# Softmax maxima taken off by one product per head, and expert results kept in the order of the tokens' place in SBUF, on one Trainium2 core

## The chip, the cores and the metric

One core of one Trainium2 chip runs the whole program in one launch. The metric is the device time of that launch in microseconds; of the kernel before there are three runs, and the median counts.

## The reference

The input `x` is (2, 1024, 128) in f32. It passes a pre-norm attention block and a pre-norm mixture of experts, each added to its input.

- Attention: layernorm, RMS norm with a weight, then q, k and v for 16 heads of 8. One half of the output is causal linear attention over features of q and k of degree two, `y / (z + eps)`. The other half is softmax attention in which query t sees the keys t-64 to t. Both halves are joined and multiplied by `Wout` (256 x 128).
- Experts: layernorm, 8 gate logits, the top two experts per token with softmax weights. An expert computes `z = (x W1 + b1) * (x W2 + b2)`, `o = silu(z Wg + bg) * (z Wl + bl)`, `y = o W3 + b3`; the token's result is the weighted sum of its two experts' y.

## The kernel before

The 2048 tokens are 16 chunks of 128 (`NC`), chunk c holding tokens 128 c to 128 c + 127, one per partition: `x_all[p, c]`. After a stage of norms and projections, in which q and k are written to DRAM split into bf16 parts, there are two stages.

**Attention** goes chunk by chunk, each of four units (`u`; heads 8 at a time, window half `j = u // 2`, head half `hf = u % 2`). All five engines have hand-written streams with waits on semaphores. For each unit TensorE issues, in this order (`chunk`, from L624):

- L638: the products that update the linear attention's state (not in the last chunk of a sequence);
- L602: next unit's window scores with queries on the output's partitions, 8 products, for the maxima only. VectorE reduces them (L1098) to `mrow`: 128 partitions x 4, partition 64 r + q and column pr holding the maximum of head 2 pr + r and query q;
- `post`: the tail of the chunk before. In a chunk's first unit these are transposes of its outputs (L555, L557), which wait until ACT has copied them out of PSUM (L838, L839); later the product with `Wout` (L580, L581), the gate (L583) and places in the experts' lists (L541, L542);
- L655: the unit's scores again, now with keys on partitions, 8 products of 64 columns into bank ST, and onto them L659: minus the maxima;
- L673 and L678: linear attention. L678 waits for the squared scores that ACT makes (L818) and POOL masks (L1305);
- L614, L621: next unit's linear scores, and sums for the features;
- L690: after ACT has taken the exponential (L830) of bank ST, the products with v.

The maxima reach bank ST as a product because a value per column must be the same on all partitions. VectorE's `maxima` (L1093 to L1108) makes two bf16 parts of `-mrow`: `mneg[:, b, 0]` by L1105, the rounded value, and `mneg[:, b, 1]` by L1107, what the rounding lost. L659 then multiplies, for each of the four columns pr and each part, one column of `mneg`, repeated 128 times as weights, with a 128 x 128 identity; column k of the output gets `mneg[k]`, so 128 columns are the 64 queries of two heads. That is 4 x 2 = 8 products of 128 columns per unit, 512 in all.

VectorE, in the same chunk, does divisions, the second layernorm and the routing (`post`, from L1018): top two experts of each token (L1057 to L1074), one-hot rows (L1084), `member` (L1088), and `weights_row`, which writes into a token's row its weights and the number of the row where the result is to go (L1000): `tokid` for the first expert and `tokid + N` for the second (L986). POOL, besides the masks, multiplies features (L1260) and scatters the tokens' rows to DRAM, each to its expert's region of `routed` (L1266), two scatters per chunk. The first of them is issued in the chunk's last unit.

**Experts**: 39 tiles of 128 rows (`NT = 39`; each expert has at least one, and 31 are placed by a table that VectorE computes after the last token is routed, L1151 to L1171). `run_steps` fixes the order: tiles 0 to 7 are the first tiles of experts 0 to 7, the other 31 follow by the table. SP loads a tile's rows (`load_tile`), after the eighth tile only when the table is there and the regions' ends are padded (L470). Per step the engines work on five tiles at once: TensorE L720 to L753, VectorE L1188 to L1217, ACT L860 to L879. POOL scatters a tile's 128 weighted results as rows of 512 B into `results` (L1327), a tensor of two halves of N = 2048 rows. VectorE takes a slot's row numbers anew (L1216, L1217) only after the scatter that used it has landed.

**The end**: SP waits for all scatters (L475), issues eight loads of 256 KB (L479; four groups of four chunks, both halves), VectorE adds the two halves (L1223) and then `x_all` (L1225), and SP stores each group (L482).

## Time and profile before

| | |
|---|---|
| median of three runs | 466.5 us (466.21, 466.5, 468.2) |
| the profiled execution | 469.27 us, of which span 467.1 us |
| attention's units | from about 50 to 271 us |
| routing's last rows, table, first tiles | about 271 to 311 us |
| experts | to 452 us |
| last scatter's landing, loads, additions, stores | 453.5 to 467.1 us |

A line of the timeline is a group of instructions merged where they follow each other: start, length, engine, line, operation, tiles, count, and in brackets how long the engine was idle before it and what ended that. A line of waits is: who waited (engine, tile, line) for whom, us in total, how often, the longest. PE is TensorE's matmuls, PEld its weight loads, DVE is VectorE, SPq and POOLq are the parts of those engines that issue DMAs. The names in tiles are the program's tensors; `qas` also stands for the buffers that share its memory later (`og`, `oT`, `z`, `yw`), `ks` for `res`.

### The profile page before, as it was taken

What the parts mean: (1) busy time and instruction counts of PE and PEld (TensorE: products, weight loads), DVE (VectorE), ACT (ScalarE), POOL (GpSimd) and SP (SyncE); (2) the same over time, 40 slices, a digit from 0 to 9 for tenths busy, and PEclk for the clock granted to TensorE, in tenths of its full rate; (3) what the DMA queues carried; (4) which work ended last, traced back from release to release, by engine and by line L of the source; (5) the groups of instructions that cost most, each with busy time, mean ns of one, the idle gap of its engine ahead of it and who ended that gap; (6) DMA issues with size and microseconds to landing.
All of it is one profiled execution on the core that took longest, in us unless ns stands there. A gap on an engine that the chain in (4) does not pass through costs nothing. (4 is left out here: it accounts for less than half of the span.)

```text
span 467.1 us, 14166 instructions
## 1 busy us (share of the span) xinstructions
PE 392.9 (84%) x4805; PEld 265.0 (57%) x4805; DVE 292.8 (63%) x1150; ACT 204.0 (44%) x470; POOL 177.9 (38%) x305
## 2 busy tenths in 40 slices
PE   0877998999999999999999931799999999999930
PEld 0455676777766777767677620355555555555510
DVE  5566554678756877766766646267666666666614
ACT  0456454554554555554554610143444444444410
POOL 5263533454454564465553353012222222222220
PEclk9999999999999999999999975699999999999965
DMA  7548976555575555333324600201111111111008
GB/s 212 134 123 171 194 176 108 134 152 142 155 160 129 138 147 145 105 77 72 79 56 150 174 27 25 82 25 48 39 38 33 32 35 37 34 32 37 17 20 254
DMA packets 91623, 46.13 MB, mean 99 GB/s; under 512 B 56410, under 2 KB 89852, under 8 KB 91554
## 3 DMA queue, kind: packets, MB, share of 16 engines
q1 hardware_dynamic: 88562, 40.51, 34.7%
q0 software_dynamic: 2272, 4.46, 2.9%
q8 instruction: 40, 0.66, 0.6%
q10 hardware_dynamic: 720, 0.26, 0.2%
q14 instruction: 29, 0.24, 0.2%
HBM read 33.69 MB, written 11.98 MB: 98 GB/s over the span
## 5 line engine op out<-in xcount | busy, mean ns | idle before, releaser
L1327 POOL DMA_INDIRECT results<-qas,mrowid x39 | 38.1, 978 | 124.6 <-ACT qas L879 121.7
L1305 POOL TENSOR_SCALAR_AFFINE_SELECT amat<-amat 128x512 f32<-128x512 f32 x64 | 40.6, 635 | 108.9 <-ACT amat L818 108.6
L1098 DVE TENSOR_REDUCE mrow<-ps 128x4 f32<-128x512 f32 x64 | 44.1, 688 | 58.2 <-PE ps L602 58.0
L746 PE MATMUL ps<-wgl,rest 128*128 (+1 forms) x156 | 75.7, 608 | 2.8 <-DVE hT L1188 2.1
L830 ACT ACTIVATE pmat<-ps 128x512 f32<-128x512 f32 x64 | 38.2, 597 | 68.8 <-PE ps L659 68.8
L818 ACT ACTIVATE amat<-ps 128x512 f32<-128x512 f32 x64 | 38.2, 597 | 13.8 <-PE ps L614 10.6
L1188 DVE TENSOR_TENSOR hT<-ps,kv_tok 128x512 f32<-128x512 f32 x39 | 27.0, 691 | 26.5 <-PE ps L746 15.5
L731 PE MATMUL ps<-w,rest 128*128 (+1 forms) x78 | 41.9, 620 | 0.0
L746 PEld LDWEIGHTS ps<-wgl,rest 128*128 128x128 f32 x156 | 27.1, 193 | 26.0 <-issue 25.7
L659 PE MATMUL ps<-identb,mneg 128*128 128x128 bf16 x512 | 39.2, 219 | 0.0
L1266 POOL DMA_INDIRECT routed<-routed_row,slot x32 | 32.6, 1018 | 14.7 <-issue 5.8
L879 ACT ACTIVATE qas<-rest,mweight 128x128 f32<-128x128 f32 x39 | 15.7, 402 | 50.3 <-DVE rest L1205 50.3
L738 PEld LDWEIGHTS ps<-kv_tok,qas 128*128 128x128 f32 x156 | 23.6, 194 | 20.1 <-issue 20.0
L1260 POOL TENSOR_TENSOR phik<-u_tok 128x128 f32<-128x128 f32 (+3 forms) x112 | 33.4, 329 | 0.0
L1200 DVE TENSOR_TENSOR hT<-ps,b 128x512 f32<-128x512 f32 x39 | 26.7, 684 | 8.0 <-PE ps L731 8.0
L1193 DVE TENSOR_TENSOR qas<-qas,hT 128x256 f32<-128x256 f32 x39 | 16.6, 425 | 21.1 <-ACT qas L873 21.1
L659 PEld LDWEIGHTS ps<-identb,mneg 128*128 128x128 bf16 x512 | 29.7, 98 | 0.0
L638 PE MATMUL ps<-v,phik 128*96 128x18 f32 x224 | 28.7, 243 | 0.4 <-POOL phik L1260 0.4
L690 PE MATMUL ps<-pmat,v 128*32 128x64 f32 x1024 | 27.6, 225 | 0.6 <-ACT pmat L830 0.4
L602 PE MATMUL ps<-ks,qas 114*64 114x128 bf16 x512 | 26.5, 225 | 1.4 <-issue 1.4
L868 ACT COPY rest<-ps 128x384 f32<-128x384 f32 (+2 forms) x41 | 19.0, 463 | 18.8 <-PE ps L724 18.8
L690 PEld LDWEIGHTS ps<-pmat,v 128*32 128x32 f32 x1024 | 17.2, 109 | 17.2 <-ACT pmat L830 14.2
(161 smaller groups left out, 821.5 us busy)
## 6 DMA issues: line engine op xcount, KB each, us to landing
qa_parts<-wgl SPq DMA_DIRECT2D x12, 256.0 KB, 3.2
ks<-k_parts SPq DMA_DIRECT2D x32, 96.0 KB
qas<-qa_parts SPq DMA_DIRECT2D x32, 96.0 KB
xin<-routed SPq DMA_DIRECT2D x39, 72.0 KB, 1.9
ks<-k_parts SPq DMA_DIRECT2D x32, 64.0 KB
qas<-qa_parts SPq DMA_DIRECT2D x32, 64.0 KB
w<-in_W SPq DMA_DIRECT2D x2, 1024.0 KB, 5.7
wgl<-in_Wg SPq DMA_DIRECT2D x2, 1024.0 KB, 6.2
```

The source lines that it names most:

```text
L638: t = mm(ps[0:PR, KV, 2 * at * UD:2 * (at + 1) * UD], phik[:, p, 2 * at:2 * at + 2, :].rearrange("p h f -> p (h f)"), v1[:, p, 1, j, :].re ...
L659: t = mm(ps[:, ST, pr * CH:(pr + 1) * CH], mneg[:, u % 2, part, pr:pr + 1].to_broadcast([128, 128]), identb[:], start=False, stop=(part == ...
L690: t = mm(ps[32 * g:32 * g + 32, bank, at:at + WINDOW], slot32(v1[:, p, j], 8 * hf + hh), pmat[:, u % 2, hh, :], start=False, stop=True, sk ...
L731: mm(ps[:, X12, :], zxT[:, (k + 1) % 2, 2, :], rhs(w12[:, bass.ds(expert(1), 1), :]), start=True, stop=True).then_inc(x12_ready, 1)
L746: t = mm(ps[:, GL, :], zxT[:, k % 2, s, :], rhs(wgl[:, bass.ds(e, 1), s, :]), start=(s == 0), stop=(s == 1))
L818: a_(amat[:, u % 2].rearrange("p g t -> p (g t)"), ps[:, A, :], ACT.Square).then_inc(square_done, 1)
L830: a_(pmat[:, u % 2].rearrange("p g t -> p (g t)"), ps[:, ST, :], ACT.Exp).then_inc(exp_done, 1)
L1098: v.tensor_reduce(mrow[:], ps[:, SQ, :].rearrange("p (a k) -> p a k", k=CH), AX.X, ALU.max).then_inc(max_done, 1)
L1260: t = q.tensor_tensor(phik[:, p, :, at:at + w], u_tok[:, :, 0:w], u_tok[:, :, dl:UD], ALU.mult)
L1266: q.indirect_dma_start(routed, bass.IndirectOffsetOnAxis(slot[:, b, k:k + 1], 0), routed_row[:, b, :], None).then_inc(scattered[b], 16)
L1305: q.affine_select(out=amat[:, u % 2], in_=amat[:, u % 2], compare_op=ALU.is_ge, fill=0.0, base=0, pattern=[[0, 4], [1, CH]], channel_multi ...
L1327: q.indirect_dma_start(results, bass.IndirectOffsetOnAxis(mrowid[:, m:m + 1], 0), yw[:, m, :], None, bounds_check=RESULTS - 1, oob_is_err= ...
```

## The change

Maxima: `mneg` is now indexed by buffer, column pr and half r, with 128 partitions. The rows of a column (pr, r) hold, on the 64 partitions of half r, the rounded maxima of head 2 pr + r, and on the other 64 what the rounding lost. One product with `minusid`, two negated 64 x 64 identities on top of each other, adds both parts for one head: eight products of 64 columns per unit. VectorE makes `mneg` by two copies and two subtractions, each on 64 partitions, of which the subtractions write to the other half.

Results: `tokid` is now 16 p + c instead of 128 c + p, so the rows of `results` have the order of `x_all`'s places, partition by partition. A token's row in the second half is now the one for the expert with the higher number (`higher`), no longer the one for its second choice.

Tiles: 0 to 6 are the first tiles of experts 0 to 6, the table's 31 follow, and the last tile (38) is the first tile of expert 7. The wait for the table and for the padding comes one tile earlier.

End: SP waits for all scatters but the last tile's, loads half 0 in four loads, waits for the last, loads half 1 in four. VectorE adds half 0 to `x_all` by groups, then half 1.

```diff
--- before.py
+++ after.py
@@ -83,7 +83,7 @@
     valid[::T // CH, :, :WINDOW] = BIG
     c["iota8"] = np.tile(np.arange(E, dtype=np.float32), (128, 1))
     c["region0"] = np.tile(np.arange(E, dtype=np.float32) * REGION, (128, 1))
-    c["tokid"] = (np.arange(CH)[:, None] + CH * np.arange(NC)[None]).astype(np.float32)
+    c["tokid"] = (NC * np.arange(CH)[:, None] + np.arange(NC)[None]).astype(np.float32)
     pad = np.zeros((CH, ROW), np.float32)
     pad[:, D + E:] = TOPK * N + np.arange(CH)[:, None]
     c["padrows"] = pad
@@ -94,7 +94,7 @@
     c["sums"] = sums.reshape(KR, 2 * PR).astype(bf)
     c["qrows"], c["arows"], c["krows"] = (x.reshape(KR - KP, H * CH).astype(bf) for x in (qrows, arows, krows))
     c["valid"] = valid.reshape(NC, H * CH).astype(bf)
-    c["identb"] = np.eye(128, dtype=np.float32).astype(bf)
+    c["minusid"] = np.tile(-np.eye(WINDOW, dtype=np.float32), (2, 1)).astype(bf)
     return c
 
 
@@ -124,7 +124,7 @@
         results = dram("results", (RESULTS, D))
 
         ident = sb("ident", [128, 128])
-        identb = sb("identb", [128, 128], BF16)
+        minusid = sb("minusid", [128, WINDOW], BF16)
         sums = sb("sums", [KR, 2, PR], BF16)
         blockdiag = sb("blockdiag", [D, D])
         statemask = sb("statemask", [PR, 8 * UD])
@@ -167,7 +167,7 @@
         v1 = sb("v1", [CH, 2, 2, 2, SLOTW])
         state = sb("state", [PR, 2, 2, CH])
         mrow = sb("mrow", [128, 4])
-        mneg = sb("mneg", [128, 2, 2, 4], BF16)
+        mneg = sb("mneg", [128, 2, 4, 2], BF16)
         phiq = sb("phiq", [PR, 2, 4, CH])
         amat = sb("amat", [CH, 2, 4, CH])
         pmat = sb("pmat", [CH, 2, 8, WINDOW])
@@ -195,6 +195,7 @@
         top = sb("top", [CH, 8])
         topi = sb("topi", [CH, 8], mybir.dt.uint32)
         topf = sb("topf", [CH, 2])
+        higher = sb("higher", [CH, 1])
         onehot = sb("onehot", [CH, 2, E])
         member = sb("member", [CH, E], BF16)
         gap = sb("gap", [CH, 1])
@@ -280,7 +281,7 @@
          oT_copied, y_ready, y_added, y_weighted) = (sem(n) for n in (
              "tzx_ready", "zx_copied", "x12_ready", "x12_added", "z_ready", "meta_copied", "gl_ready", "gl_added",
              "silu_done", "o_ready", "to_ready", "oT_copied", "y_ready", "y_added", "y_weighted"))
-        res_in = [sem(f"res_in{g}") for g in range(NG)]
+        res_in = [[sem(f"res_in{k}{g}") for g in range(NG)] for k in range(2)]
         res_sum, out_sum = sem("res_sum"), sem("out_sum")
 
         TZX, X12, Y, TO, GL = SQ, ST, A, PHI, OUT0
@@ -317,12 +318,12 @@
 
             def expert_of(t):
 
-                if t < E:
-                    return t
+                if t < E - 1 or t == NT - 1:
+                    return min(t, E - 1)
                 if t not in known:
-                    if t == E:
+                    if t == E - 1:
                         engine.wait_ge(table_ready, 1)
-                    known[t] = engine.value_load(table[0:1, 0, t - E:t - E + 1], min_val=0, max_val=E - 1)
+                    known[t] = engine.value_load(table[0:1, 0, t - E + 1:t - E + 2], min_val=0, max_val=E - 1)
                 return known[t]
 
             known = {}
@@ -366,7 +367,7 @@
                 sp.dma_start(as_[KP:KR, p], con["arows"]).then_inc(s_in, 16)
                 for w in range(2):
                     sp.dma_start(ks[KP:KR, p, w], con["krows"]).then_inc(s_in, 16)
-            for dst, name in ((identb, "identb"), (sums, "sums"), (statemask, "statemask"), (epslin, "epslin")):
+            for dst, name in ((minusid, "minusid"), (sums, "sums"), (statemask, "statemask"), (epslin, "epslin")):
                 sp.dma_start(dst[:].rearrange("r a f -> r (a f)") if name == "sums" else dst[:], con[name]).then_inc(c_in, 16)
 
             def router_in():
@@ -455,28 +456,33 @@
                 if j >= 4:
                     sp.wait_ge(tzx_ready, j - 1)
                     sp.wait_ge(meta_copied, j - 3)
-                if j < E:
-                    row = j * REGION
+                if j < E - 1 or j == NT - 1:
+                    row = min(j, E - 1) * REGION
                 else:
-                    row = sp.value_load(table[0:1, 1, j - E:j - E + 1], min_val=0, max_val=E * REGION)
+                    row = sp.value_load(table[0:1, 1, j - E + 1:j - E + 2], min_val=0, max_val=E * REGION)
                 sp.dma_start(xin[:, k, :], routed[bass.ds(row, CH), :]).then_inc(xin_ready[k], 16)
 
             for j in range(4):
                 load_tile(j, j)
             pad_regions(sp)
-            for j in range(4, E):
+            for j in range(4, E - 1):
                 load_tile(j, j % 4)
             sp.wait_ge(table_ready, 1)
             sp.wait_ge(padded, 16 * (E + 1))
-            for j in range(E, NT):
+            for j in range(E - 1, NT):
                 load_tile(j, j % 4)
 
+            def load_results(half):
+                for g in range(NG):
+                    at = slice(g * GC, (g + 1) * GC)
+                    sp.dma_start(res[half][:, at], results[half * N:(half + 1) * N].rearrange("(p c) d -> p c d", c=NC)[:, at]).then_inc(res_in[half][g], 16)
+
+
             for k in range(4):
-                sp.wait_ge(y_out[k], 16 * ((NT - k + 3) // 4))
-            for g in range(NG):
-                for k in range(2):
-                    lo = k * N + g * GT
-                    sp.dma_start(res[k][:, g * GC:(g + 1) * GC], results[lo:lo + GT, :].rearrange("(c p) d -> p c d", p=CH)).then_inc(res_in[g], 16)
+                sp.wait_ge(y_out[k], 16 * ((NT - 1 - k + 3) // 4))
+            load_results(0)
+            sp.wait_ge(y_out[(NT - 1) % 4], 16 * ((NT - 1) // 4 + 1))
+            load_results(1)
             for g in range(NG):
                 sp.wait_ge(out_sum, g + 1)
                 sp.dma_start(out.rearrange("b (c p) d -> p (b c) d", p=CH)[:, g * GC:(g + 1) * GC], x_all[:, g * GC:(g + 1) * GC]).then_inc(done, 16)
@@ -654,10 +660,9 @@
                         h = 8 * hf + hh
                         mm(ps[:, ST, hh * WINDOW:(hh + 1) * WINDOW], ks[:, p, j, h, :], qs[:, p, h, j * WINDOW:(j + 1) * WINDOW],
                            start=(hh == 0), stop=False, skip_group_check=True)
-                    for pr in range(4):
-                        for part in range(2):
-                            t = mm(ps[:, ST, pr * CH:(pr + 1) * CH], mneg[:, u % 2, part, pr:pr + 1].to_broadcast([128, 128]), identb[:],
-                                   start=False, stop=(part == 1), skip_group_check=True)
+                    for hh in range(8):
+                        t = mm(ps[:, ST, hh * WINDOW:(hh + 1) * WINDOW], mneg[:, u % 2, hh // 2, hh % 2:hh % 2 + 1].to_broadcast([128, 128]), minusid[:],
+                               start=False, stop=True, skip_group_check=True)
                     t.then_inc(st_ready, 1)
 
                     bank = OUT0 + pair % 2
@@ -983,7 +988,7 @@
                 n, b = r + 1, r % 2
                 dve.wait_ge(r_egap, n)
                 v.tensor_scalar(wsum[:], egap[:], 1.0, None, ALU.add).then_inc(r_ws, 1)
-                v.tensor_scalar(tmp8[:, 1], onehot[:, 1], float(N), None, ALU.mult).then_inc(r_tmp, 1)
+                v.tensor_scalar(tmp8[:, 1], iota8[:], higher[:, 0:1], float(N), ALU.is_equal, ALU.mult).then_inc(r_tmp, 1)
                 dve.wait_ge(r_ws, n)
                 v.reciprocal(w01[:, 0:1], wsum[:]).then_inc(r_w, 1)
                 dve.wait_ge(r_w, n)
@@ -1082,7 +1087,8 @@
                             dve.wait_ge(r_row, n - 1)
                         for s in range(2):
                             v.tensor_scalar(onehot[:, s], iota8[:], topf[:, s:s + 1], None, ALU.is_equal).then_inc(r_oh, 1)
-                        dve.wait_ge(r_oh, 2 * n)
+                        v.tensor_tensor(higher[:], topf[:, 0:1], topf[:, 1:2], ALU.max).then_inc(r_oh, 1)
+                        dve.wait_ge(r_oh, 3 * n)
                         if c > 2:
                             dve.wait_ge(pos_ready, n - 1)
                         v.tensor_tensor(member[:], onehot[:, 0], onehot[:, 1], ALU.add).then_inc(r_member, 1)
@@ -1102,10 +1108,14 @@
                 if not isinstance(n, int) or n > 1:
 
                     dve.wait_ge(st_ready, n - 1)
-                v.tensor_scalar(mneg[:, b, 0], mrow[:], -1.0, None, ALU.mult).then_inc(nh_done, 1)
-                dve.wait_ge(nh_done, n + 1)
-                v.scalar_tensor_tensor(out=mneg[:, b, 1], in0=mrow[:], scalar=-1.0, in1=mneg[:, b, 0],
-                                       op0=ALU.mult, op1=ALU.subtract).then_inc(mneg_ready, 1)
+
+                half = [slice(0, WINDOW), slice(WINDOW, 2 * WINDOW)]
+                for r in range(2):
+                    v.tensor_copy(mneg[half[r], b, :, r], mrow[half[r]]).then_inc(nh_done, 1)
+                dve.wait_ge(nh_done, 2 * (n + 1))
+                for r in range(2):
+                    t = v.tensor_tensor(mneg[half[1 - r], b, :, r], mrow[half[r]], mneg[half[r], b, :, r], ALU.subtract)
+                t.then_inc(mneg_ready, 1)
 
             def chunk(c, p, i):
                 later, kf = folded(c)
@@ -1219,10 +1229,13 @@
             run_steps(dve, step, (-2, -1, 1))
             for g in range(NG):
                 at = slice(g * GC, (g + 1) * GC)
-                dve.wait_ge(res_in[g], 32)
-                v.tensor_tensor(res[0][:, at], res[0][:, at], res[1][:, at], ALU.add).then_inc(res_sum, 1)
+                dve.wait_ge(res_in[0][g], 16)
+                v.tensor_tensor(x_all[:, at], x_all[:, at], res[0][:, at], ALU.add).then_inc(res_sum, 1)
+            for g in range(NG):
+                at = slice(g * GC, (g + 1) * GC)
+                dve.wait_ge(res_in[1][g], 16)
                 dve.wait_ge(res_sum, g + 1)
-                v.tensor_tensor(x_all[:, at], x_all[:, at], res[0][:, at], ALU.add).then_inc(out_sum, 1)
+                v.tensor_tensor(x_all[:, at], x_all[:, at], res[1][:, at], ALU.add).then_inc(out_sum, 1)
 
         @block.gpsimd
         def _(pool):
```

## Rows read from the trace of the kernel before

**Rows 1.** The page, part 1: busy time of each engine, its share of the span, instructions.

```profile
PE 392.9 (84%) x4805; PEld 265.0 (57%) x4805; DVE 292.8 (63%) x1150; ACT 204.0 (44%) x470; POOL 177.9 (38%) x305
```

**Rows 2.** By stretches, attention: length; PE, PEld, DVE, ACT, POOL busy; PEclk; DMA share; GB/s.

```profile
100.00:200.00 100.00, 94.46 (x1836) 71.79 (x1833) 72.53 (x341) 52.32 (x121) 53.32 (x110) 1.00 0.53 139
```

**Rows 3.** Groups of instructions in attention, 75 to 270 us: busy us, mean ns, idle before.

```profile
L659 PE MATMUL ps<-identb,mneg 128*128 128x128 bf16 x448 | 34.3, 219 | 0.0
...
L655 PE MATMUL ps<-qas,ks 114*128 114x64 bf16 x448 | 22.4, 193 | 0.0
...
L1105 DVE TENSOR_SCALAR mneg<-mrow 128x4 bf16<-128x4 f32 x55 | 10.4, 189 | 1.1
...
L1084 DVE TENSOR_SCALAR onehot<-iota,topf 128x8 f32<-128x8 f32 x28 | 5.5, 242 | 0.0
```

**Rows 4.** Timeline of a chunk's third unit: start us, us, instruction group.

```profile
196.09 0.39 PE L655 MATMUL ps<-qas,ks 114*128 114x64 bf16 x8
...
196.32 0.61 PE L659 MATMUL ps<-identb,mneg 128*128 128x128 bf16 x8
...
196.97 0.60 ACT L830 ACTIVATE pmat<-ps 128x512 f32<-128x512 f32 x1 [1.64 <-PE ps L659]
...
197.77 0.43 PE L690 MATMUL ps<-pmat,v 128*32 128x64 f32 x16
197.79 0.36 DVE L1084 TENSOR_SCALAR onehot<-iota,topf 128x8 f32<-128x8 f32 x2
```

**Rows 5.** Waits in attention, 75 to 270 us: us in total, times, longest.

```profile
DVE mrow L1098 <- PE ps L602: 47.2, 39, 2.5
...
ACT linT L838 <- PE ps L690: 7.3, 9, 0.8
```

**Rows 6.** Timeline of a boundary between chunks, where ACT's copy waits.

```profile
186.50 0.43 PE L690 MATMUL ps<-pmat,v 128*32 128x64 f32 x16
...
186.80 1.07 POOL L1266 DMA_INDIRECT routed<-routed_row,slot  x1 [0.19 <-issue]
...
188.03 0.27 ACT L838 COPY linT<-ps 128x128 f32<-128x128 f32 x1 [0.78 <-PE ps L690]
...
188.52 0.44 PE L555 MATMUL ps<-ident,linT 128*128 128x128 f32 x2 [0.80 <-ACT winT L839]
```

**Rows 7.** Timeline of another boundary, where it does not wait.

```profile
158.62 0.43 PE L690 MATMUL ps<-pmat,v 128*32 128x64 f32 x16
...
159.37 1.07 POOL L1266 DMA_INDIRECT routed<-routed_row,slot  x1 [0.20 <-issue]
...
159.77 0.44 PE L555 MATMUL ps<-ident,linT 128*128 128x128 f32 x2
...
160.47 0.65 POOL L1305 TENSOR_SCALAR_AFFINE_SELECT amat<-amat 128x512 f32<-128x512 f32 x1
...
161.28 0.41 PE L678 MATMUL ps<-amat,v 128*32 128x128 f32 x8
```

**Rows 8.** The experts' stage, 311 to 448 us: waits; then the DMA view, KB each, us to landing.

```profile
DVE mweight L1216 <- DMA results<-qas,mrowid: 4.5, 10, 0.9
...
results<-qas,mrowid POOLq DMA_INDIRECT x39, 2.4
```

**Rows 9.** The end: timeline, then the chain of waits, then the table by stretches.

```profile
448.73 0.98 POOL L1327 DMA_INDIRECT results<-qas,mrowid  x1 [2.69 <-ACT qas L879]
...
453.61 5.42 SPq L479 DMA_DIRECT2D ks<-results  x8
...
451.34 2.12 DMA results<-qas,mrowid
...
457.97 5.09 DMA ks<-results
...
463.81 0.69 DVE x_all L1225
...
457.80:464.50 6.70, 0.00 (x0) 0.00 (x0) 5.48 (x8) 0.00 (x0) 0.00 (x0) 0.50 1.01 295
```

## The prediction

> **What bounds the kernel now.** I read the page first: TensorE is busy for 84% of the span of 467.1 us, VectorE 63% [rows 1]. The profiled execution took 469.27 us, 2.77 us above the median of the three runs (466.5); I work out differences in its trace and take them off that median. A difference of 0.5% (2.3 us) is about what a measurement of this kernel can tell from no change.
>
> The table by stretches comes next, because the change touches attention and the end, not the middle. In attention TensorE is busy 94% of the time, VectorE 73%, and no other engine much above half [rows 2]: here the bound is the in-order stream of TensorE. The reader is to look at starts, not at durations, since matmuls overlap: one 64-column product lasts 193 ns and one 128-column product 219 ns [rows 3], yet eight of the first (L655) fill 0.39 us, so they start (0.39-0.19)/7 = 0.029 us apart, and eight of the second (L659) fill 0.61 us, or (0.61-0.22)/7 = 0.056 us apart [rows 4]. Both load 128 columns of bf16 weights, so the pitch goes by the streamed columns, not by the load.
>
> **Part 1, stacked maxima, TensorE.** Eight products of 128 columns per unit become eight of 64, with weights of the same size. If they keep L655's pitch, a unit saves 8 x (0.056-0.029) = 0.21 us; over 64 units that would be 13.6 us. It counts only where TensorE's own stream is what ends the unit. The exponential (L830) follows L659 and L690 follows it 0.2 us after its end [rows 4]; both move with L659, so that chain gives the saving through. This holds for the two middle units of all 16 chunks: 32 units.
>
> At a chunk's boundary (last unit, first unit of the next) it does not. In nine of the 15 boundaries ACT's copy L838 waits up to 0.8 us for L690 [rows 5], though L690 should be over: in one of them L690 starts at 186.50 and the copy only at 188.03, just after POOL's scatter L1266 (186.80 to 187.87), and L555 starts 2.02 us after L690 [rows 6]. In a boundary where the scatter started 0.75 us behind L690, not 0.30, there was no such hold and L555 came 1.15 us after L690 [rows 7]. The scatter's start hangs on POOL's chain from the unit before, which L659 does not touch. So with the hold as it is, the savings of both units are swallowed; with L690 0.21 us further ahead of the scatter it may get clear of it, and then a boundary gains 2.02-1.15 = 0.87 plus 0.42, 1.3 us. Bounds 0 and 1.3 for each of nine; the new distance, 0.51 us, is halfway between the held and the free row, and behind the first scatter comes a second that may hold the same stream. I take 0.45, a third of the way. The other 14 units save 0.21 us unless POOL's mask ends too late: in the free boundary L1305 ended at 161.12 and L678 started at 161.28 [rows 7], so there only some 0.1 us is left to gain. I count ten of 14. Sum: 42 x 0.21 + 9 x 0.45 = 8.8 + 4.1 = 12.9 us.
>
> **Part 1, VectorE.** Two small operations, the first of 0.19 us [rows 3], become four, two on each half of the partitions. Nothing in the trace is of this form. Below, the second of a pair overlaps the first, as in the pair L1084, where two of 0.24 us [rows 3] fill 0.36 [rows 4]: 0.12 each; above it runs after the first, about 0.19 each. That is 0.24 to 0.38 us per unit. I take 0.38, the end that weighs more, and cost it at nothing, because before its reduction VectorE waits for TensorE 47.2 us in 55 units, 0.86 us a unit [rows 5], and the minus maxima are used only a unit later. Without that cover it would be 64 x 0.38 = 24 us.
>
> The Trainium skill, page "VectorE: DVE Perf Modes", section "Two Vector instructions with no wait between them", says that an instruction whose operands start in another quadrant of partitions than the last ones waits until all earlier Vector instructions have finished. That would be the upper of the two bounds; no row of this trace shows it, and the sum is the same by either.
>
> **Part 2, order of results' rows.** A token's row is now 16 x partition + chunk, so a load brings each partition one run of 2 KB, not four rows of 512 B. The scatters L1327 write as many rows as before, spaced differently. They land 2.4 us after issue, and VectorE waited for them ten times, 4.5 us in all [rows 8]. Nothing shows what a wider spacing costs; from 4.5 us less to the rival below, I take zero: the size of a written row is unchanged.
>
> **Part 3, the end.** Row halves now go by the higher expert, the last tile is expert 7's first, and so half 0 is loaded once tile 37 has landed. `higher` adds one small operation per chunk, under VectorE's idle time, except in the last two chunks' drain: 0.2 us, which the range takes in. Tile 7's row is read from the table and its load now stands behind the pad writes on SP; they are issued well before VectorE lets tile 7's slot go. Before: the last scatter starts at 451.34 and lands 2.12 us later; SP issues eight loads from 453.61; the last lands at 463.06, then two additions of 0.7 us and the store, end at 467.1 [rows 9]. After: the scatter of tile 37 started at 448.73, 2.61 us earlier, and the first load goes out that much earlier. During 457.8 to 464.5 the DMA engines are full at 295 GB/s [rows 9], so the 9.45 us from first issue to last landing stay, or shrink with the longer runs: bounds 0 and 1.5 us, I take 0.5, near the row's own rate, since that share is already 1. Four additions move into the wait: 0.7 us off the path. Sum 2.6+0.5+0.7 = 3.8 us (2.6 to 4.8).
>
> Together 16.7 us: 466.5-16.7 = 449.8.
>
> **Rivals.**
> A. *The hold goes away in most boundaries*: 9 x 1.3 for 4.1, 7.6 us more: 442. For it: the free boundary [rows 7]. Against: the second scatter. 0.2.
> B. *The hold stays with all its cost* (boundaries give nothing): 4.1 us less, 454. With part 3 at its lower bound and fewer free units, 457. 0.17.
> C. *The weight load is what limits the products*: each of them still loads 128 columns, and halving the streamed ones does nothing. Then only part 3 is left, 462.7. Against it: L655's pitch with the same weights [rows 4]; for it only that its weights are one repeated column, which L655's are not. 0.05.
> The Trainium skill, page "TensorE: Matmul & The Clock Gate", section "LDWEIGHTS (loading the stationary operand)", gives a load P/1.2 ns, 107 ns for 128 columns. By that neither group could go at the pitch the trace shows, so the trace speaks against it here, and the chance stays low.
> D. *VectorE becomes the bound*: decides if its queue is over 0.86 us a unit later; 0.38 added and 0.21 less cover leave 0.27. If half of the units lose 0.2 us, 6 us: 456. 0.05.
> E. *Slower*: the results' rows, now 8 KB apart for neighbouring tokens, land later. VectorE may reuse a slot only when its scatter has landed; at 2.4 us it waits ten times [rows 8], above about 3.3 us every second tile pays all of the excess. One us more than that is about 20 us over 18 pairs: 470. Against: a run is 512 B in both. 0.04.
>
> **How the numbers follow.** The forecast as such has 0.49, A 0.2, B 0.17, C 0.05, D 0.05, E 0.04. The range leaves out C, E and the ends of A and B: 441 to 458.5. Faster by over 0.5% is all but E and mishaps of the same kind: 0.94; within 0.5% 0.02; slower 0.04.
>
> **What would show it.** Eight products of the new line in about 0.40 us; middle units 0.2 us shorter; ACT's wait for L690 at boundaries gone or fewer than nine (A), or as it is (B); VectorE's wait for L602 down to roughly 25 us; the first load of results before the last scatter, and at most 8.5 us from the last scatter's landing to the end. It is wrong if the new products still fill 0.6 us, or if the waits for scatters in the experts' stage grow.

## The result, and the profile after

Four runs of each, in turn on one chip: the kernel before 467.05 us median (466.21 to 468.2), the changed one 461.6 us (460.85 to 463.04), a ratio of 0.987, 95% interval 0.982 to 0.992. That is 5.5 us less, where 16.7 had been forecast, and it lies above the predicted range. The profiled execution took 463.04 us, with a span of 461.3 (before 469.27 and 467.1).

The page, part 1:

```profile
PE 379.9 (82%) x4805; PEld 253.7 (55%) x4805; DVE 333.9 (72%) x1294; ACT 204.0 (44%) x470; POOL 179.7 (39%) x305
```

The table by stretches, attention, columns as in [rows 2]:

```profile
100.00:200.00 100.00, 90.37 (x1864) 68.00 (x1861) 92.66 (x413) 52.60 (x121) 54.16 (x108) 1.00 0.51 138
```

TensorE did get its time back, 13.0 us of the span. But the two engines changed places: in attention TensorE fell from 94.5% busy to 90.4%, VectorE rose from 72.5% to 92.7%. The groups of instructions, 75 to 270 us, answer to [rows 3]:

```profile
L1104 DVE TENSOR_REDUCE mrow<-ps 128x4 f32<-128x512 f32 x54 | 37.0, 685 | 2.8 <-PE ps L608 1.8
L1117 DVE TENSOR_TENSOR mneg<-mrow,mneg 64x4 bf16<-64x4 f32 x108 | 26.0, 241 | 2.6
L1114 DVE CAST mneg<-mrow 64x4 bf16<-64x4 f32 x108 | 23.4, 217 | 2.7
L664 PE MATMUL ps<-minusid,mneg 128*128 128x64 bf16 x440 | 21.9, 193 | 0.0
```

L1104 is the reduction (L1098 before), L1114 and L1117 are the copies and subtractions that took the place of L1105 and L1107, L664 the new products. The waits of the same stretch:

```profile
ACT linT L843 <- PE ps L695: 8.2, 11, 1.1
PEld ps L661 <- DVE mneg L1117: 5.5, 12, 0.8
PE ps L644 <- DVE state L1134: 4.5, 9, 0.7
PE ps L661 <- DVE mneg L1117: 3.4, 10, 0.6
DVE mrow L1104 <- PE ps L608: 1.8, 4, 0.9
```

VectorE's wait for the window scores, 47.2 us in [rows 5], is down to 1.8, and TensorE waits for VectorE in its place, for the minus maxima (L661, before L655) and for the state. One unit shows it, with the third unit of [rows 4] to compare:

```profile
191.16 0.36 DVE L1114 CAST mneg<-mrow 64x4 bf16<-64x4 f32 x2
191.56 0.71 DVE L1117 TENSOR_TENSOR mneg<-mrow,mneg 64x4 bf16<-64x4 f32 x2
191.61 0.64 POOL L1318 TENSOR_SCALAR_AFFINE_SELECT amat<-amat 128x512 f32<-128x512 f32 x1 [1.26 <-ACT amat L823]
192.32 0.41 PE L661 MATMUL ps<-qas,ks 114*128 114x64 bf16 x8 [0.27 <-DVE mneg L1117]
192.56 0.40 PE L664 MATMUL ps<-minusid,mneg 128*128 128x64 bf16 x8
...
194.46 1.07 POOL L1279 DMA_INDIRECT routed<-routed_row,slot  x1 [0.20 <-issue]
194.89 0.81 DVE L1114 CAST mneg<-mrow 64x4 bf16<-64x4 f32 x2
```

L664's eight fill 0.40 us, as predicted. L661 starts when the subtractions are done. A pair of small operations fills 0.33 to 0.36 us when POOL is idle, 0.71 beside POOL's mask (L1318, before L1305) and 0.81 beside a scatter (L1279, before L1266).

A boundary between chunks, as in [rows 6]:

```profile
180.06 0.43 PE L695 MATMUL ps<-pmat,v 128*32 128x64 f32 x16
180.33 1.07 POOL L1279 DMA_INDIRECT routed<-routed_row,slot  x1 [0.20 <-issue]
181.65 0.27 ACT L843 COPY linT<-ps 128x128 f32<-128x128 f32 x1 [0.83 <-PE ps L695]
182.13 0.44 PE L561 MATMUL ps<-ident,linT 128*128 128x128 f32 x2 [0.32 <-ACT winT L844]
```

The transposes L561 (L555 before) start 2.07 us after L695 (L690 before), as they did before: the hold stands.

The end, the timeline, against [rows 9]:

```profile
445.64 0.98 POOL L1340 DMA_INDIRECT results<-qas,mrowid  x1 [2.10 <-ACT qas L884]
447.57 0.98 POOL L1340 DMA_INDIRECT results<-qas,mrowid  x1 [0.95 <-ACT qas L884]
447.84 5.54 SPq L478 DMA_DIRECT2D ks<-results  x8
455.07 2.70 DVE L1238 TENSOR_TENSOR x_all<-x_all,ks 128x512 f32<-128x512 f32 x4 [0.93 <-DMA ks<-results]
```

The chain of waits there:

```profile
447.57 4.06 DMA results<-qas,mrowid
452.96 4.10 DMA ks<-results
```

SP's first loads (L478) go out 0.27 us behind the last scatter, which lands after 4.06 us; the span ends 9.7 us later. The waits of the experts' stage, 311 to 448 us, against [rows 8]:

```profile
DVE mweight L1226 <- DMA results<-qas,mrowid: 7.7, 11, 1.8
```

The stages, from the starts and ends of rows (first L655 or its like; last product with v; first transposes of an experts' tile; last scatter's start; end of the span), in us:

| | before attention | attention | routing, table | experts | end |
|---|---|---|---|---|---|
| before | 50.9 | 219.5 | 22.6 | 158.4 | 15.8 |
| after | 49.1 | 213.7 | 22.5 | 162.4 | 13.7 |
| difference | -1.8 | -5.8 | -0.1 | +4.0 | -2.1 |

Attention gave 5.8 in place of 12.9, the end 2.1 in place of 3.8, and in this one execution the experts' stage took 4.0 of it back (in the changed kernel's other profiled execution, below, it lasted 158.4, as before). The 1.8 us ahead of attention are chance: that stage lasts between 49.0 and 51.3 us in all executions, whose code is the same there but for one constant.

### The profile page after: what moved, and what is told of

Its sections match the earlier page's. It is cut to its first block and busy times, and to the rows that moved or that the text cites. A ratio compares the mean times of both kernels' runs of the same rounds, so it can differ in the third digit from the quotient of the medians.

```text
span 461.3 us, 14314 instructions
## 1 busy us (share of the span) xinstructions
PE 379.9 (82%) x4805; PEld 253.7 (55%) x4805; DVE 333.9 (72%) x1294; ACT 204.0 (44%) x470; POOL 179.7 (39%) x305
## 5 line engine op out<-in xcount | busy, mean ns | idle before, releaser
L751 PE MATMUL ps<-wgl,rest 128*128 (+1 forms) x156 | 76.7, 615 | 6.1 <-DVE hT L1198 5.7
L1318 POOL TENSOR_SCALAR_AFFINE_SELECT amat<-amat 128x512 f32<-128x512 f32 x64 | 41.2, 644 | 93.8 <-ACT amat L823 93.3
L835 ACT ACTIVATE pmat<-ps 128x512 f32<-128x512 f32 x64 | 38.2, 597 | 63.9 <-PE ps L664 63.8
L1104 DVE TENSOR_REDUCE mrow<-ps 128x4 f32<-128x512 f32 x64 | 43.9, 686 | 9.8 <-PE ps L608 8.7
L823 ACT ACTIVATE amat<-ps 128x512 f32<-128x512 f32 x64 | 38.2, 597 | 11.6 <-PE ps L620 8.9
L1279 POOL DMA_INDIRECT routed<-routed_row,slot x32 | 32.6, 1020 | 14.5 <-issue 6.0
L1117 DVE TENSOR_TENSOR mneg<-mrow,mneg 64x4 bf16<-64x4 f32 x128 | 29.5, 230 | 3.1
L695 PE MATMUL ps<-pmat,v 128*32 128x64 f32 x1024 | 27.5, 225 | 2.9 <-ACT pmat L835 2.4
L644 PEld LDWEIGHTS ps<-v,phik 128*96 128x96 f32 x224 | 23.2, 163 | 10.8 <-issue 6.6
L1114 DVE CAST mneg<-mrow 64x4 bf16<-64x4 f32 x128 | 26.8, 209 | 3.2
L661 PE MATMUL ps<-qas,ks 114*128 114x64 bf16 x512 | 25.6, 193 | 3.5 <-DVE mneg L1117 3.4
L695 PEld LDWEIGHTS ps<-pmat,v 128*32 128x32 f32 x1024 | 17.2, 109 | 19.5 <-ACT pmat L835 17.0
```

The costliest lines, as they stand in the source:

```text
L644: t = mm(ps[0:PR, KV, 2 * at * UD:2 * (at + 1) * UD], phik[:, p, 2 * at:2 * at + 2, :].rearrange("p h f -> p (h f)"), v1[:, p, 1, j, :].re ...
L695: t = mm(ps[32 * g:32 * g + 32, bank, at:at + WINDOW], slot32(v1[:, p, j], 8 * hf + hh), pmat[:, u % 2, hh, :], start=False, stop=True, sk ...
L751: t = mm(ps[:, GL, :], zxT[:, k % 2, s, :], rhs(wgl[:, bass.ds(e, 1), s, :]), start=(s == 0), stop=(s == 1))
L823: a_(amat[:, u % 2].rearrange("p g t -> p (g t)"), ps[:, A, :], ACT.Square).then_inc(square_done, 1)
L835: a_(pmat[:, u % 2].rearrange("p g t -> p (g t)"), ps[:, ST, :], ACT.Exp).then_inc(exp_done, 1)
L1104: v.tensor_reduce(mrow[:], ps[:, SQ, :].rearrange("p (a k) -> p a k", k=CH), AX.X, ALU.max).then_inc(max_done, 1)
```

## The experiments

Theory V: VectorE bounds the changed attention, its four small operations cost far more than their free length (the length that they have when POOL does nothing beside them). Rivals: the hold at the boundaries eats the gain (T in the expectations), or the result rows or the new end cost something. H is a theory of the hold itself: the scatter beside L690 makes it. Each diff is against the kernel named; each run has six to twelve executions unless said otherwise, and every ratio is to the kernel before on the same chip.

**The maxima alone**: the kernel before with every hunk of the change that touches `minusid`, `mneg` and `maxima`.

```diff
-mneg = sb("mneg", [128, 2, 2, 4], BF16)
+mneg = sb("mneg", [128, 2, 4, 2], BF16)
...
-for pr in range(4):
-    for part in range(2):
...
+for hh in range(8):
+    t = mm(ps[:, ST, hh * WINDOW:(hh + 1) * WINDOW], mneg[:, u % 2, hh // 2, hh % 2:hh % 2 + 1].to_broadcast([128, 128]), minusid[:],
...
+    t = v.tensor_tensor(mneg[half[1 - r], b, :, r], mrow[half[r]], mneg[half[r], b, :, r], ALU.subtract)
```

> The maxima's change alone, old rows of results and old end. Theory V (VectorE has become what ends attention: two more small operations, each of the four held until the one before is over): attention (first scores L655 to the last L690) takes about 214 us as in the changed kernel, against 219.5 before, VectorE busy over 90% of 100 to 200 us; the whole 460 to 463. Theory T (TensorE's saving is eaten at the chunk boundaries by POOL's scatters, VectorE only looks busy): the same total, but the middle units keep their full 0.21 us and VectorE's waits for L602 stay above 25 us. The experts' stage takes as long as before (158 us from the first transpose to the last scatter) if the new order of rows is what slowed it in the changed kernel, 162 if the order has nothing to do with it.

462.64 us (461.72 to 464.42), ratio 1.014 (1.011 to 1.018): slower by 1.4%. And this chip's kernel before took 455.9 us, not 467. The waits of the run, 75 to 255 us:

```profile
PEld ps L655 <- DVE mneg L1110: 10.1, 19, 1.0
PE ps L655 <- DVE mneg L1110: 6.4, 12, 0.9
DVE mrow L1097 <- PE ps L602: 4.2, 4, 2.1
```

The groups of VectorE there:

```profile
L1110 DVE TENSOR_TENSOR mneg<-mrow,mneg 64x4 bf16<-64x4 f32 x104 | 30.4, 293 | 2.5
L1107 DVE CAST mneg<-mrow 64x4 bf16<-64x4 f32 x104 | 23.0, 221 | 2.6
```

One unit's subtractions, timeline:

```profile
180.99 0.64 POOL L1308 TENSOR_SCALAR_AFFINE_SELECT amat<-amat 128x512 f32<-128x512 f32 x1 [1.16 <-ACT amat L817]
181.02 0.93 DVE L1110 TENSOR_TENSOR mneg<-mrow,mneg 64x4 bf16<-64x4 f32 x2
182.00 0.41 PE L655 MATMUL ps<-qas,ks 114*128 114x64 bf16 x8 [0.58 <-DVE mneg L1110]
```

The pair starts just behind POOL's mask and ends 0.32 us after it, and TensorE waits 0.58 us for the pair. Two findings at once: TensorE's loss to VectorE is larger than its gain, as V says, and this chip's before is 11 us faster than the first one's, so something is different in it.

**The rows and the end without the maxima**: the kernel after with those hunks undone.

```diff
-for hh in range(8):
+for pr in range(4):
+    for part in range(2):
...
+v.tensor_scalar(mneg[:, b, 0], mrow[:], -1.0, None, ALU.mult).then_inc(nh_done, 1)
```

> The order of rows and the new end alone, old maxima. If the end is worth what it showed in the changed kernel (2.05 us from last scatter to end) and the experts' stage stays at its length: 465. If the new order of rows slows the scatters: experts' stage 4 us longer, whole 467 to 469. If neither slows: 463 with the 3.8 us that the prediction gave the end.

456.02 us (452.47 to 458.61), ratio 1.000 (0.997 to 1.003). Last scatter to end took 14.1 us, two less than in the kernel before, and yet nothing is left of it.

**Four products, no small operations**: the kernel after, in which the reduction itself writes the maxima as bf16.

```diff
-v.tensor_reduce(mrow[:], ps[:, SQ, :].rearrange("p (a k) -> p a k", k=CH), AX.X, ALU.max).then_inc(max_done, 1)
+v.tensor_reduce(mneg[:, b], ps[:, SQ, :].rearrange("p (a k) -> p a k", k=CH), AX.X, ALU.max).then_inc(max_done, 1)
...
-    v.tensor_copy(mneg[half[r], b, :, r], mrow[half[r]]).then_inc(nh_done, 1)
...
-    t = v.tensor_tensor(mneg[half[1 - r], b, :, r], mrow[half[r]], mneg[half[r], b, :, r], ALU.subtract)
...
+for pr in range(4):
+    t = mm(ps[:, ST, pr * CH:(pr + 1) * CH], mneg[:, u % 2, pr:pr + 1].to_broadcast([128, 128]), minusid[:],
```

`minusid` is a negated 128 x 128 identity here. The low part of the maxima is left out; what rounding takes off a query's scores is the same for all its keys and leaves again in the division by the sum.

> The changed kernel with the lower part of the maxima left out (the rounded maximum is subtracted; it cancels in the division): the reduction writes bf16 itself, and four products of 128 columns with a negated identity add it. TensorE's work in these products is four pitches of 0.056, 0.22 us, as in the changed kernel's eight of 64, but VectorE has no small operation at all in place of four. Theory V: attention falls to the 12.9 us below before that the prediction had, or more: 203 to 207 us, the whole 448 to 454. Theory T: attention stays at 213 to 215, the whole 460 to 462.

442.54 us (439.53 to 447.31), ratio 0.968 (0.963 to 0.973), and on another chip:

> The kernel with four products and no small operation on VectorE, once more. It took 442.5 against 455.9 before (ratio 0.968). If this call's chip shows the hold (before at 466 to 468): theory V says the ratio is the same or lower, 448 to 453; if the holds swallow the boundaries' share, 453 to 456. Without the hold: 442 again.

442.97 us (439.77 to 448.9), 0.968 (0.963 to 0.973). The first run's table by stretches:

```profile
100.00:200.00 100.00, 99.50 (x1947) 74.31 (x1947) 72.92 (x331) 59.66 (x141) 60.98 (x123) 1.00 0.60 147
```

A unit's products, timeline:

```profile
187.41 0.40 PE L660 MATMUL ps<-qas,ks 114*128 114x64 bf16 x8
187.64 0.39 PE L663 MATMUL ps<-minusid,mneg 128*128 128x128 bf16 x4
```

VectorE's wait, 75 to 255 us:

```profile
DVE mneg L1104 <- PE ps L607: 42.3, 33, 2.8
```

The products fill 0.39 us as the eight of the change do, VectorE is back at 73% with 42.3 us of waiting, TensorE at 99.5%, and attention takes 195.5 us. With products of the same length and VectorE's work gone, attention is 12.4 us shorter than the 207.9 us of the kernel before on such a chip (measured below), where 64 x 0.21 = 13.4 were to be had. That settles V: it is VectorE's part of the change that keeps the saving back. This version beats both kernels.

**The two operations on halves, old products**: the kernel before, with

```diff
-v.tensor_scalar(mneg[:, b, 0], mrow[:], -1.0, None, ALU.mult).then_inc(nh_done, 1)
+for r in range(2):
+    v.tensor_scalar(mneg[half[r], b, 0], mrow[half[r]], -1.0, None, ALU.mult).then_inc(nh_done, 1)
...
+for r in range(2):
+    t = v.scalar_tensor_tensor(out=mneg[half[r], b, 1], in0=mrow[half[r]], scalar=-1.0, in1=mneg[half[r], b, 0],
...
```

> The kernel before, its products too, but each of the two small operations split into two on 64 partitions, as in the change (no write to the other half). It has the change's load on VectorE without its saving on TensorE. Theory V: VectorE is pushed to its limit, attention gets 2 to 8 us longer, the whole 469 to 475. Theory T: nothing moves, 466 to 468. By durations: if each operation is held until the one before is over, a pair fills 0.33 us; if they overlap, 0.24.

458.32 us (456.84 to 464.31), 1.007 (1.004 to 1.010), attention 210.4 us. With TensorE's products unchanged, two more operations on VectorE cost 2.5 us of attention (207.9 in the kernel before on such a chip, below).

**The same four operations, on two of the four columns and all partitions**, against the run above:

```diff
-half = [slice(0, WINDOW), slice(WINDOW, 2 * WINDOW)]
+half = [slice(0, 2), slice(2, 4)]
...
-    v.tensor_scalar(mneg[half[r], b, 0], mrow[half[r]], -1.0, None, ALU.mult).then_inc(nh_done, 1)
+    v.tensor_scalar(mneg[:, b, 0, half[r]], mrow[:, half[r]], -1.0, None, ALU.mult).then_inc(nh_done, 1)
...
```

The second operation is changed in the same way.

> The kernel before and its products, with each of the two small operations split into two of two columns on all 128 partitions: as many operations as with halves, but none that changes its partitions. If the change of partitions holds an operation until the one before is over, a pair fills 0.24 us here against 0.33 with halves, and the kernel stays within 1 us of before, where the halves cost 2.4 us. If it is only the number of operations, the pair fills 0.33 here too and the cost is the same 2.4 us.

467.82 us (466.45 to 470.48), 1.001 (0.998 to 1.004), on a chip whose before takes 467.99. The two ratios, 1.007 and 1.001, are not to be set against each other: they are from unlike chips, and on this one VectorE has more idle time to spare (in the kernel before it waits 47.0 us for L602, 75 to 270 us, against 35.8 on a chip like that of the halves). What can be compared are the operations themselves. VectorE's rows of both runs, first columns, then halves:

```profile
200.73 0.24 DVE L1108 TENSOR_SCALAR mneg<-mrow 128x2 bf16<-128x2 f32 x2
201.00 0.23 DVE L1111 SCALAR_TENSOR_TENSOR mneg<-mrow,mneg 128x2 bf16<-128x2 f32 x2
```

```profile
194.68 0.73 DVE L1111 SCALAR_TENSOR_TENSOR mneg<-mrow,mneg 64x4 bf16<-64x4 f32 x2
195.35 0.65 POOL L1310 TENSOR_SCALAR_AFFINE_SELECT amat<-amat 128x512 f32<-128x512 f32 x1
...
196.24 0.36 DVE L1108 TENSOR_SCALAR mneg<-mrow 64x4 bf16<-64x4 f32 x2
196.64 0.33 DVE L1111 SCALAR_TENSOR_TENSOR mneg<-mrow,mneg 64x4 bf16<-64x4 f32 x2
```

Two operations on all partitions overlap and fill 0.24 us; on different halves the second starts when the first has ended, 0.36. Four on columns cost 0.47 us a unit, four on halves 0.69 free. This is what the Trainium skill, page "VectorE: DVE Perf Modes", section "Two Vector instructions with no wait between them", says of a change of quadrant; the prediction had it unconfirmed, and these rows agree with it.

**Other operations in the four places**, against the maxima alone:

```diff
-    v.tensor_copy(mneg[half[r], b, :, r], mrow[half[r]]).then_inc(nh_done, 1)
+    v.tensor_scalar(mneg[half[r], b, :, r], mrow[half[r]], 1.0, None, ALU.mult).then_inc(nh_done, 1)
...
-    t = v.tensor_tensor(mneg[half[1 - r], b, :, r], mrow[half[r]], mneg[half[r], b, :, r], ALU.subtract)
+    t = v.scalar_tensor_tensor(out=mneg[half[1 - r], b, :, r], in0=mrow[half[r]], scalar=1.0, in1=mneg[half[r], b, :, r],
...
```

> The maxima's change alone, with the two copies written as multiplications by one and the two subtractions as scalar_tensor_tensor: same data, same partitions, other kinds of operation. In the kernel with the maxima alone the subtractions took 505 ns in the mean where POOL's mask ran beside them and 160 ns where nothing did; with halves that write to their own half as scalar_tensor_tensor it was 192. If the kind of operation makes VectorE wait for POOL: these fall to about 200 and the kernel is 3 to 6 us faster than with the maxima alone (1.000 to 1.005 of before without the hold). If it is the write to the other half, or only when they come: they stay near 400 to 500 and the ratio near 1.014.

462.81 us (461.64 to 463.83), 1.014 (1.011 to 1.018). The kind of operation is not it.

**The subtractions into their own half**, against the maxima alone:

```diff
-v.tensor_tensor(mneg[half[1 - r], b, :, r], mrow[half[r]], mneg[half[r], b, :, r], ALU.subtract)
+v.tensor_tensor(mlost[half[r], b, :, r], mrow[half[r]], mneg[half[r], b, :, r], ALU.subtract)
```

`mlost` is read by nobody and `mneg` is zeroed once, so the low part of the maxima is left out here too.

> The maxima's part alone, as in the run of the maxima alone, but with the two subtractions writing to their own half of the partitions, in a tensor that nobody reads; the halves that the product takes in beside the rounded maxima are set to zero once, so the low part of the maxima is left out, which the division by the sum takes out again. VectorE issues the same four small operations per unit, TensorE the same products. If it is the writing to the other half that lets a subtraction wait for POOL (K, for crossing): a subtraction beside POOL's mask takes 0.16 to 0.25 us in place of 0.5, the group of subtractions has a mean under 200 ns (319 for it in the run of the maxima alone), attention gets 5 to 9 us shorter than with the crossing, and the time is 0.99 to 1.005 of the kernel before. If any operation on half of the partitions waits for POOL (P), the mean stays over 280 ns and the ratio at 1.01 to 1.018, as for the maxima alone (1.014).

461.91 us (460.87 to 466.68), 1.015 (1.008 to 1.021), and in 75 to 255 us:

```profile
L1111 DVE TENSOR_TENSOR mlost<-mrow,mneg 64x4 bf16<-64x4 f32 x105 | 31.0, 295 | 2.5
```

295 ns against 293 (the expectation's 319 is a slip; the row of the maxima alone says 293): K fell, the crossing costs nothing.

**The columns of a half side by side**, against the maxima alone, and against the whole change:

```diff
-mneg = sb("mneg", [128, 2, 4, 2], BF16)
+mneg = sb("mneg", [128, 2, 2, 4], BF16)
...
-    v.tensor_copy(mneg[half[r], b, :, r], mrow[half[r]]).then_inc(nh_done, 1)
+    v.tensor_copy(mneg[half[r], b, r], mrow[half[r]]).then_inc(nh_done, 1)
...
```

> The maxima's part alone, with the four columns of one half laid side by side in the tensor of the minus maxima (buffer, half, column in place of buffer, column, half): each of VectorE's four small operations then reads and writes four neighbouring bf16 numbers, where it took every second one; the subtractions cross to the other half as in the change. Same products, same number of operations. If it is the spaced bf16 numbers that let these operations wait for POOL (S): those beside POOL's mask take 0.16 to 0.25 us, the group of subtractions has a mean under 220 ns (293 for the maxima alone), attention gets 5 to 9 us shorter than 215 and the time is 0.99 to 1.005 of the kernel before. If it is the half of the partitions as such, or only where in POOL's operation they fall (P): a mean over 270 ns, attention near 215 us, ratio 1.008 to 1.018 on a chip whose kernel before takes 456 us.

> The whole changed kernel with that layout. S: ratio to the kernel before 0.99 to 1.005 where that takes 456 us, 0.97 to 0.98 where it takes 467. P: 1.008 to 1.018 at 456 us, 0.983 to 0.99 at 467, as the change itself.

463.14 us (460.86 to 466.11), 0.987 (0.984 to 0.990), and 462.62 us (460.95 to 465.04), 0.987 (0.985 to 0.990), on a chip whose before takes 468.58. The subtractions' mean was 229 ns and 228 ns, attention 215.2 and 214.1 us. Neither S (under 220) nor P (over 270) has its number. But on such a chip the change itself has 241 (the group above), and a subtraction that starts while POOL's mask runs takes 526 ns in this layout and 532 in the change's (means), so S fell as well: the times are those of P. A second reading matters more: the maxima alone, 1.4% slower on one chip, are in this layout 1.3% faster on this one, and attention takes 215 us on both. What differs is the kernel before.

**Beside which of POOL's operations.** I sorted all 128 subtractions of the maxima alone by what POOL does when they start, from the starts and ends in the trace. In 32 the mask runs already: they take 483 to 640 ns (mean 576), and every one of them ends 11 to 26 ns after the mask. Of the others, 74 start with POOL idle (mean 159), 12 beside the products L1263 (271), 7 beside a scatter (160) and 3 beside L1293 (159); the 13 among all these during which the mask starts take 157 to 160. So it is the order of the two that counts, and it is the rest of the mask that is waited for. Of the copies, the 33 that start beside a scatter take 152 to 846 ns (mean 334), the 86 with POOL idle 165.

The number of subtractions that start in the mask also explains the two means above: 32 of 128 in the maxima alone (293 ns), 24 in the change (241), 22 in the layout side by side (229).

The Trainium skill, page "SBUF — State Buffer", section "Who interferes with whom", says that a Vector instruction with two inputs in SBUF contends with a GpSimd instruction that reads SBUF, a copy in a two-port mode with GpSimd, and that whoever comes first blocks the other. The sorted durations agree with all three: the subtractions have two inputs and wait beside the mask and the products, the copies wait beside the scatter, and a subtraction that is ahead of the mask is as short as a free one. In the kernel before the same kinds of operation are short because they seldom come second: of its 64 second operations (L1107) none starts in the mask, of the first (L1105) two do, and one of these takes 543 ns. That they keep clear of it because VectorE waits for TensorE ahead of each reduction is argued, not tried.

**The changed kernel and the kernel before again**, nothing edited, where the kernel before takes 467.99 us (of the latter one execution, with a profile).

> The changed kernel, once more. Where the kernel before takes 456: theory V gives 458 to 462 (the maxima alone took 462.6 there, the rows and the end nothing), so the change makes it slower by 0.5 to 1.5%; theory T gives 450 to 453. Where the kernel before takes 467: 461 to 463 as measured.

> The kernel before, once more, for its trace on the chip of this call. Beside it the runs of the kernel before have taken 466 to 468 us in one place and 453 to 460 in another. If what differs is the hold at the chunk boundaries (L690 late by 1.1 us where POOL scatters), this trace shows L555 1.15 us after L690 in all boundaries where it takes 456, and 2.05 us in nine of them where it takes 467; attention 209 and 219 us. If it is anything else, the boundaries look alike in both.

After: 461.27 us (459.23 to 464.55), ratio 0.987 (0.984 to 0.990), attention 216.4; VectorE's wait for L608 is 3.2 us. Before: 469.15 us, attention 218.8, nine boundaries held. And where the kernel before takes 456.04 us:

> The kernel before once more, to see on this chip whether the nine boundaries are held. The hold belongs to the chip: with a median near 467 nine boundaries have L555 2.0 us after L690, with a median near 456 none has (all 1.13 to 1.15).

456.59 us, attention 207.9. The same boundary in both, first at 469.15 us, then at 456.59:

```profile
186.10 0.43 PE L690 MATMUL ps<-pmat,v 128*32 128x64 f32 x16
186.41 1.07 POOL L1266 DMA_INDIRECT routed<-routed_row,slot  x1 [0.20 <-issue]
187.67 0.27 ACT L838 COPY linT<-ps 128x128 f32<-128x128 f32 x1 [0.82 <-PE ps L690]
```

```profile
180.20 0.43 PE L690 MATMUL ps<-pmat,v 128*32 128x64 f32 x16
180.51 1.07 POOL L1266 DMA_INDIRECT routed<-routed_row,slot  x1 [0.20 <-issue]
180.84 0.26 ACT L838 COPY linT<-ps 128x128 f32<-128x128 f32 x1
181.35 0.44 PE L555 MATMUL ps<-ident,linT 128*128 128x128 f32 x2
```

Same code, same distance of 0.31 us from L690 to the scatter, and ACT goes on 1.57 us after L690 or 0.64 us after it. As far as these few chips tell, the hold belongs to the chip: on three chips the kernel before takes 456 us, and no trace of a kernel with the old products has a held boundary (on one of them the trace is that of the kernel before itself); on one, met twice, it takes 468, with nine held; the first comparison, 467, shows nine too. It is worth the 11 us of attention between 218.8 and 207.9.

**The first scatter a unit earlier**, twice against the kernel before, once against the four products:

```diff
-if u == (2 if c == NC else 3) and has[3] and c - 3 < NC - 2:
+if u == 2 and has[3] and c - 3 < NC - 2:
```

> The kernel before with POOL's first scatter of a chunk issued in the third unit and no longer in the fourth; nothing else moves. Theory H (where the kernel before takes 467, TensorE's stream is held for about a microsecond by the scatter that starts while L690 runs at the boundary): the late L690 goes from all nine boundaries and L555 follows it by 1.15 us; how much of the 10 us comes back depends on what the scatter then meets: 458 if nothing waits for it there, 464 to 467 if it holds the third unit instead. If the hold belongs to the place and not to the scatter: nine boundaries stay at 2.05 us. Where the kernel before takes 456, no change under either.

> The kernel before with each chunk's first scatter issued by POOL one unit earlier, in the chunk's third unit, on whatever chip this is. Where the kernel before shows the hold (its L690 in a chunk's last unit ends 1.1 us late, median about 467 us): if the scatter's start beside the products causes the hold (H), the boundaries with L555 2.05 us after L690 go from nine to at most two, attention gets 6 to 10 us shorter and the time is 0.980 to 0.987 of the kernel before; unless the scatter holds the products of the third unit in its place, then no change, 0.995 to 1.005. If the hold has another cause than the scatter (O), nine boundaries stay held and the ratio is 0.995 to 1.003. On a chip without the hold (median about 456 us) all say 0.995 to 1.002, as once already.

> The changed kernel with VectorE's small operations taken out altogether: the reduction writes the maxima rounded to bf16, four products of 128 columns take them off (the low part is left out, and goes out again in the division), and the first scatter of a chunk is issued in the third unit. VectorE bounds the change (V): 13 to 15 us under the kernel before on a chip without the hold, ratio 0.965 to 0.972, as with the four products alone. On a chip with the hold, and H true: a further 5 to 10 us less, ratio 0.945 to 0.96; H false: 0.965 to 0.98.

454.57 us (453.18 to 457.32), 0.997 (0.995 to 1.000); 454.38 us (453.38 to 457.41), 0.998 (0.995 to 1.002); with the four products 444.19 us (441.01 to 452.88), 0.968 (0.962 to 0.975). All three met chips without the hold, where theory and rival say the same. So H is untried where it counts, and what makes the hold stays open. Three things in the traces speak for the scatter without proving it. On the held chip the first three boundaries, where POOL scatters nothing yet, are free (L555 1.15 to 1.22 us after L690), and so is the one with the scatter 0.75 us behind. And on the free chips there is a small hold too: with the four products the scatter starts 0.49 to 0.54 us behind the products with v, whose semaphore comes 0.14 to 0.25 us later than behind a free group; with the scatter a unit earlier, in the last of these runs, it comes at those boundaries as behind a free group.

**The rows alone**, the kernel before with

```diff
-c["tokid"] = (np.arange(CH)[:, None] + CH * np.arange(NC)[None]).astype(np.float32)
+c["tokid"] = (NC * np.arange(CH)[:, None] + np.arange(NC)[None]).astype(np.float32)
...
+sp.dma_start(res[k][:, g * GC:(g + 1) * GC], results[k * N:(k + 1) * N].rearrange("(p c) d -> p c d", c=NC)[:, g * GC:(g + 1) * GC]).then_inc(res_in[g], 16)
```

and **the end alone**, the rows and the end without the maxima, with the rows' order of before:

```diff
+sp.dma_start(res[half][:, at], results[half * N + g * GT:half * N + (g + 1) * GT].rearrange("(c p) d -> p c d", p=CH)).then_inc(res_in[half][g], 16)
```

> The new order of the results' rows alone, old end and old maxima. Its loads bring 2 KB runs. If longer runs help: from the first load's issue to the last landing 8.7 us or less, against 9.45 before, the whole 0.5 to 1 us faster. If writing rows 8 KB apart costs: scatters land later than 2.4 us in the median, and the experts' stage (first transpose to last scatter) is longer than before by 1 to 4 us.

> Old maxima and old order of rows, with the new halves, the new order of tiles and the early loads. From last scatter to end about 14 us against 16 before, as with both. If the experts' stage gives that back because of the order of tiles (a real tile at the end, a table tile in place 7), the steps after the eighth add up to 8 us above 3.57 each, against 6.6 with the old order of tiles, and the whole is within 1 us of before; if it was the order of rows, they add up to 6.6 and the whole is 2 us faster.

Rows alone 467.58 us (465.17 to 471.49), 1.000 (0.997 to 1.003), with a median landing of the scatters of 2.6 us (2.4 before) and 4.0 us of waiting for them on VectorE (4.5 before). End alone 455.62 us (452.53 to 459.09), 1.001 (0.998 to 1.005). Neither is worth anything that can be measured. The end does get shorter: over the twelve profiled executions with the old end it takes 15.5 to 16.8 us (mean 15.9), over the eight with the new one 13.2 to 15.1 (mean 13.9). But the experts' stage has a mean of 158.7 us with the old order of tiles (157.8 to 159.7) and 160.3 with the new one (158.4 to 162.4). The order alone was not run; that it takes back most of the 2 us rests on these means, whose spreads overlap, and the one execution of the end alone does not show it (158.6 us, with an end of 15.1).

## Why the prediction was right and wrong

**Right.** The bound before was TensorE's stream, and the price of the products was right: eight of 64 columns fill 0.40 us, rival C fell. The saving of 0.21 us a unit is real too: with VectorE's work out of the way it gave 207.9 - 195.5 = 12.4 us of attention on chips without the hold, against 64 x 0.21 = 13.4 (the prediction has 13.6 there). Rows at zero: right, and rival E fell; VectorE's wait for scatters grew from 4.5 to 7.7 us (5.7 in the second execution), which the prediction had as a sign against it, but with the rows alone it was 4.0 and the time the same.

**The step that failed** is "VectorE", where I took 0.38 us a unit "and cost it at nothing, because before its reduction VectorE waits for TensorE 47.2 us in 55 units". Two things are wrong in it. The size: the groups give (241 + 217) x 2 = 0.92 us a unit where L1105 and L1107 took 0.36, so 0.56 more; the page says the same, VectorE's busy time rose by 41.1 us (292.8 to 333.9), of which `higher` is 2.9, so 38.2 / 64 = 0.60 each. The free part of it, 0.69 - 0.36 = 0.33, lies within the forecast's bounds of 0.24 to 0.38; the other 0.23 to 0.27 come from POOL, and no bound held them (sorted as above, the 24 subtractions that start in the mask and the 28 copies that start beside a scatter are 532 and 355 ns long, 0.37 and 0.19 us over the free length, together 0.22 a unit). And the cover: 0.86 us a unit was counted with the hold in it, in which VectorE waited too, and it had to pay for the 0.21 us by which the unit gets shorter. 0.60 + 0.21 = 0.81 leaves almost nothing of it. Without the hold the cover is 35.8 us in 55 units, 0.65 a unit, and 0.81 is more than that. So rival D, given 0.05, was the case: VectorE sets attention at 213.7 to 216.4 us, whatever the kernel before takes. D's own time, 456, was missed too, since it kept the rest of the forecast.

**The hold** stays as in rival B: eight boundaries have L561 1.97 to 2.10 us after L695, two more 1.68 and 1.87. The 4.1 us taken for them were not there. The step before that failed as well: L690's like was to come 0.21 us further ahead of the scatter, 0.51 us; in the change, where it waits for VectorE, the distance is 0.22 to 0.27 at these eight, and only the four products have the 0.53. But B's own sum, 454 to 457, does not hold either, since the middle units gave little. That the change is faster at all on the first chip fits the following, which is argued: TensorE waits at the boundaries anyway and VectorE catches up there, so the hold costs the change next to nothing (attention 214.7 to 215.1 us in the three runs of its maxima on chips without it, 213.7 to 216.4 with it) and the kernel before 11 us. On a chip without the hold the maxima are a loss of 1.4%. My chance of 0.04 for slower had no case for that: it took the one chip's profile for the kernel's.

**The end**: 3.8 us predicted, 2.1 measured. The head start of 2.61 us was the distance of two scatters before; after, they are 1.93 us apart, and the first load went out 0.27 us behind the last scatter, not ahead of it. The last scatter, beside four loads, landed after 4.06 us in place of 2.12, so half 1 waited. From its landing to the end 9.7 us passed, not 8.5. In the changed kernel's second execution it went otherwise: there the scatter before the last landed after 3.23 us in place of 2.14, the first load went out 1.43 us behind the last scatter, which then landed after 2.28, and the end took 14.4 us. And the new order of tiles, which I moved at no cost, may have given up to 1.6 us back, which no run of it alone shows.

## What to carry to other kernels

When an engine off the critical path gets more small work, its idle time is cover only by what is left after the main stream gets shorter, and a small operation is not priced by its free length: look at what POOL is already doing when it starts. First look for a form that spares that engine its work: here four products of 128 columns, with no operation of VectorE to prepare them, filled the same 0.39 us as eight of 64 columns that need four (it can be done because what rounding takes off cancels in the division). And read the kernel before on more than one chip, since a stall that one chip shows may hide the cost of the change.

## What the runs showed of the hardware

- VectorE: a pair of small operations on all partitions 0.24 us, on different halves 0.36, beside POOL's mask or scatter up to 0.93 for the pair, with single ones of up to 0.64 (subtraction, mask) and 0.85 (copy, scatter) in place of 0.16. A subtraction that starts while the mask runs ends 11 to 26 ns after it (32 of 32); one that is ahead of the mask takes its free 159 ns.
- A hold of about 0.9 us of the in-order stream of TensorE, where a scatter of POOL starts 0.3 us behind the group L690, on one chip and not on three others, worth 11 us of 467.
- In the change the late end of L695 goes with the distance. By its semaphore a free group ends 0.47 us after its start; with the scatter 0.22 to 0.27 us behind that start it is 1.0 to 1.1 us later, with 0.45 to 0.47 us 0.5 later. Why this chip holds and others don't is open.
- A scatter with four loads of 256 KB issued 0.3 to 1.7 us behind it landed after 4.06 us, alone after 2.12.
